# Gated delta-rule attention and expert feed-forward on one core: the correction of a 128x128 inverse summed in the PSUM bank of its first product

## The chip, the cores and the metric

One core of one Trainium2 chip. The metric is the device time of one execution in microseconds (us). The kernel before took 1452.8 us (median of 3 runs, 1451.58 to 1452.94).

## The reference, cut to what matters

Tokens: 2 sequences of 512, 256 features each. A gated delta-rule attention with 16 key heads and 32 value heads of width 128, then a layer norm, a feed-forward of 12 experts (3 chosen per token), and a second layer norm. The attention projects, convolves over 4 taps, applies SiLU, normalises q and k, and runs per value head the recurrence

```
St = St * exp(g_t)
kv = k_t . St
delta = (v_t - kv) * beta_t
St = St + k_t (outer) delta
o_t = q_t . St
```

and then multiplies the normalised output by SiLU(z) and projects it with W_out.

## The kernel before, in words

The kernel walks over 16 "pairs" (one key head n with its two value heads). The recurrence is done in chunks of 128 tokens: 2 sequences x 4 chunks x 2 value heads = 16 matrices (index u) of 128x128 per pair. For each a unit triangular matrix A (strictly lower part in `aT`, split in a float16 high part `aH` and a low part `aL`) has to be inverted. That is done in groups g of four matrices (0 to 3) or halves h of eight:

- steps `st`, `x0`, then five levels of `y`, `p`, `turn` build an approximate inverse `X0` and its transpose `Z0` in float16;
- `res` (L633) forms the residual of that inverse in a PSUM bank, with 12 matmuls; ScalarE takes its high part `res0` (L873), VectorE its low part `res1` (L1083);
- `once` (L645) multiplies `res0` by `Z0`, four matmuls into a bank of its own; ScalarE copies it to SBUF as float16 (L877) and the bank is free;
- `Z` (L654) sums in another bank, for each of the four matrices, `res0 x once`, `res1 x Z0`, `res0 x Z0` and `Z0` itself (through an identity): 16 matmuls at lines 660 to 663; ScalarE copies the sum into `Z` (L881).

`Z` is then used by `solve` (L697), on the chain `ks`, `solve`, `su`, `ks` of the next chunk, which carries the state `St` from chunk to chunk. `pdl`, `qs` give the output, `z` (L666) is the projection of the gate, which ScalarE evacuates with a SiLU (L885), `weigh` multiplies on VectorE, `high` and `low` split the product in two float16 parts, `oT` turns it by DMA, `op` (L725) is the output projection, added up by VectorE. Front of a pair: `proj` (L521) fills the fixed banks 0 and 1, ScalarE copies with the last tap (L788), and `tap` on VectorE adds the other three (L1016); `silu`, `tok`, `v`, `kT`, `kk`, `decay`, `aT`, `unit`, `aH`, `aL` follow. `sq1` are eight small squares on ScalarE (L815).

The order of all of it is written out by hand. `FIRST` covers the start up to pair 0's end, `ORDER` is repeated 12 times (for w = 1 to 12, with steps of pairs w, w+1 and w+2 in one copy), `LAST` covers pairs 13 to 15. Every engine goes through the same list and does those steps that are its own, in that order, so each queue is in order; between engines semaphores decide. `BANK` gives each step that writes PSUM one of the banks 2 to 7. A bank has two semaphores: `full` (TensorE has filled it) and `free` (it has been evacuated). Before a step fills its bank, `take` makes TensorE wait until all earlier uses of this bank in the list are free:

```
            b, k = place(n, step, x)
            if after(k, 1):
                pe.wait_ge(free[b], k)
```

A later step that has been taken by TensorE's queue stands behind that wait. `is_free(..., taking=...)` waits for other steps' evacuations (the data), leaving out those of the bank being taken. DMA loads of weights are issued by SyncE in list order, and wait for the splits of the weights before.

In `ORDER` before, TensorE's sequence around the gate projection is: `tok` 0, `tok` 1, `turn` (4,0) (bank 2), `z` 0 (bank 3), `z` 1 (bank 4), `z` 2 (bank 7), `y` (4,1) (bank 2), `turn` (3,1), `proj` 3, `p` (4,1), `kT` 0, `z` 3, and around the correction: `res` 0, `op` 0, `proj` 0, `once` 0, `res` 1, `op` 1, `res` 2, `Z` 0, `once` 2, `op` 2, `decay` 1, `op` 3, then the next copy with `kk` 0, `kk` 1, `Z` 2, `once` 1, `res` 3, `kk` 2, `solve` 0, `decay` 2, `Z` 1, `st` 0 (bank 2, which is also that of `res` 3), `su` 0, `st` 1, `pdl` 0, `decay` 3, `ks` 1. ScalarE's is `proj` 2, `sq1`, `turn` (4,0), `z` 0, `z` 1, `silu` 2. VectorE's at the start of the copy is `kk` 0, `aT` 0, `kk` 1, `aT` 1, `split` z, `split` out, `res` 3, `kk` 2, `st` 0, `su` 0.

After the attention the feed-forward runs (from some 1100 us on); the change does not touch it.

Of the kernel before, what the change touches and what calls it, by code (L numbers as in the profile page):

```python
# [14 lines left out]
P = 128  # L15
# [52 lines left out]
    (1, "p", (3, 1)), (2, "tap", 2), (2, "sq1", 1), (0, "weigh", 0),
    (2, "tok", 0), (2, "tok", 1), (1, "turn", (4, 0)), (0, "z", 0),
    (0, "z", 1), (2, "silu", 2), (0, "high", 0), (0, "z", 2),  # L70
    (0, "low", 0), (0, "low", 1), (0, "oT", 3), (1, "y", (4, 1)),
    (0, "weigh", 1), (1, "turn", (3, 1)), (2, "proj", 3), (1, "p", (4, 1)),
    (0, "high", 1), (2, "kT", 0), (0, "z", 3), (2, "kT", 1),
    (2, "v", (0, 1)), (2, "tap", 3), (1, "turn", (4, 1)), (2, "silu", 3),
    (2, "v", (0, 0)), (0, "weigh", 2), (0, "weigh", 3), (0, "high", 2),
    (1, "res", 0), (0, "high", 3), (0, "op", 0), (2, "proj", 0),
    (1, "once", 0), (2, "tap", 0), (1, "res", 1), (0, "op", 1),
    (0, "low", 2), (0, "low", 3), (1, "res", 2), (1, "Z", 0),
    (1, "once", 2), (1, "kd", 1), (2, "silu", 0), (1, "aL", 3),
# [50 lines left out]
    (1, "silu", 1), (0, "aL", 2), (0, "p", (4, 0)), (0, "norm", 0),  # L130
    (1, "gl", 1), (0, "y", (3, 1)), (0, "split", "out"), (1, "proj", 2),
    (1, "sq1", 1), (0, "aL", 3), (0, "p", (3, 1)), (0, "kd", 1),
    (1, "silu", 2), (0, "pT", 3), (1, "tap", 2), (1, "tok", 0),
# [3 lines left out]
    (1, "unit", 1), (0, "turn", (4, 0)), (1, "pT", 1), (0, "res", 0),  # L137
    (0, "res", 1), (0, "turn", (4, 1)), (0, "res", 2), (1, "aL", 0),
    (1, "kT", 0), (0, "split", "z"), (1, "silu", 3), (2, "load", "qkv"),
    (0, "once", 0), (1, "tap", 0), (1, "proj", 0), (0, "once", 1),  # L140
# [1765 lines left out]
```

## Time and profile before

| | |
|---|---|
| median of 3 runs | 1452.8 us |
| the profiled execution's own time | 1452.13 us |
| its span | 1450.4 us |
| TensorE (PE) busy | 1386.4 us, 96% of the span |
| VectorE (DVE) busy | 1085.8 us, 75% |
| ScalarE (ACT) busy | 1049.7 us, 72% |
| GpSimd (POOL) busy | 697.1 us, 48% |
| mean granted TensorE clock | 0.982 |
| one middle pair, from 834.41 to 898.32 us | 63.91 us |

A matmul is pipelined: its row in the trace lasts longer than the time until the next one starts, so a busy TensorE may still be issuing slower than it could, and what a matmul costs is read from start to start. Times in the rows are us from the start of the span.

### The profile page before, as it was taken

To read this page: it belongs to the slowest core of one execution; us is meant where nothing else is said; L and a number is where in the kernel's file an instruction comes from. 1 tells how busy PE (TensorE), PEld (TensorE's weight loads), DVE (VectorE), ACT (ScalarE), POOL (GpSimd) and SP (SyncE) were. 2 spreads that over 40 slices of the span, in tenths; PEclk is the share of its full clock that TensorE was granted. 3 is DMA by queue.
4 is the path that set the end of the run, shared out by engine and by line. 5 is a ranking of instruction groups with operands and counts; after the bars stand their busy time and mean duration, and the time that the engine had idled before them with its cause. 6 is when DMAs were issued, how large, how long until landed. Compare 5 with 4: busy or idle time off the path is not lost.

```text
span 1450.4 us, 36480 instructions
## 1 busy us (share of the span) xinstructions
PE 1386.4 (96%) x14236; PEld 1114.9 (77%) x14236; DVE 1085.8 (75%) x1926; ACT 1049.7 (72%) x2114; POOL 697.1 (48%) x619
## 2 busy tenths in 40 slices
PE   5689999999999999999999999999978999999996
PEld 3568888898888889798888979888865567667676
DVE  5678999999999999999999999998865512213225
ACT  5777887878788787878888887887755465564651
POOL 0545555446564545556454555545315454353440
PEclk8899999999999999999999999999998999999998
DMA  3000202011020211102030110201131112112100
GB/s 118 16 1 2 67 3 58 24 38 38 24 60 2 60 24 38 38 25 59 2 60 18 44 38 24 60 2 39 32 101 39 56 37 73 38 37 73 37 1 29
DMA packets 100992, 55.76 MB, mean 38 GB/s; under 512 B 74572, under 2 KB 93016, under 8 KB 100824
## 3 DMA queue, kind: packets, MB, share of 16 engines
q1 hardware_dynamic: 100824, 53.43, 14.2%
q8 instruction: 116, 1.90, 0.5%
q14 instruction: 52, 0.43, 0.1%
HBM read 35.59 MB, written 1.05 MB: 25 GB/s over the span
## 4 chain that ended last, share of the span: by engine, by line
PE 89%; DVE 5%; ACT 2%; issue 2%; DMA 1%; POOL 0%; SPq 0%; POOLq 0%; DVEq 0%; ACTq 0%
PE bank L532 11%; PE bank L1486 11%; PE bank L1469 11%; PE bank L687 6%; PE bank L733 5%; PE bank L674 5%; PE bank L704 4%; PE bank L722 4%; PE bank L713 3%; PE bank L622 2%; PE bank L614 2%; PE bank L630 2%; PE bank L582 2%; PE bank L558 2%; PE bank L583 2%; DVE con L1023 2%
## 5 line engine op out<-in xcount | busy, mean ns | idle before, releaser
L1023 DVE SCALAR_TENSOR_TENSOR con<-bank,taps,con 128x1022 f32<-128x1022 f32 (+2 forms) x192 | 245.4, 1278 | 19.9 <-ACT con L802 15.3
L1808 POOL TENSOR_TENSOR h<-h 128x512 f16<-128x512 f32 x120 | 142.5, 1192 | 159.7 <-ACT h L1586 147.7
L532 PE MATMUL bank<-x,qkv 128*128 128x512 f16 x768 | 183.5, 390 | 6.5 <-DVE con L1023 6.5
L1179 POOL TENSOR_TENSOR gl<-const_sb,gc 128x512 f16<-128x512 f32 x128 | 129.9, 1040 | 120.3 <-DVE gc L1033 75.2
L1585 ACT ACTIVATE h<-bank,b 128x512 f32<-128x512 f32 x120 | 82.5, 687 | 119.0 <-PE bank L1469 115.8
L1469 PE MATMUL bank<-y,w 128*128 128x512 f16 x720 | 163.2, 386 | 1.7 <-ACT h L1586 1.4
L1486 PE MATMUL bank<-w,h 128*128 128x256 f16 x1440 | 159.9, 273 | 0.0
L1486 PEld LDWEIGHTS bank<-w,h 128*128 128x128 f16 x1440 | 140.9, 98 | 18.4
L532 PEld LDWEIGHTS bank<-x,qkv 128*128 128x128 f16 x768 | 73.4, 100 | 88.5 <-issue 8.7
L1469 PEld LDWEIGHTS bank<-y,w 128*128 128x128 f16 x720 | 70.2, 99 | 90.6 <-ACT h L1586 8.1
L1214 POOL TENSOR_TENSOR oo<-oo 128x512 f16<-128x512 f32 x64 | 74.2, 1170 | 122.0 <-ACT oo L930 122.0
L1081 DVE TENSOR_TENSOR X<-X,bank 128x512 f16<-128x512 f16 x160 | 109.0, 682 | 16.1 <-PE bank L622 14.7
L1399 DVE SCALAR_TENSOR_TENSOR w<-w,w 128x1280 f16<-128x1280 f32 x12 | 17.8, 1490 | 134.1 <-ACT w L1387 134.1
L871 ACT ACTIVATE Z<-bank 128x512 f16<-128x512 f32 x160 | 96.4, 604 | 23.7 <-PE bank L630 23.7
L1072 DVE TENSOR_TENSOR Y<-bank,ymask 128x512 f16<-128x512 f32 x160 | 109.4, 685 | 2.9 <-PE bank L614 2.3
L802 ACT ACTIVATE con<-bank,taps 128x512 f32<-128x512 f32 x128 | 85.4, 687 | 30.8 <-PE bank L532 30.6
L1206 POOL TENSOR_TENSOR kd<-k_tok,gc 128x512 f32<-128x512 f32 x48 | 50.0, 1043 | 112.0 <-PE bank L713 112.0
L733 PE MATMUL bank<-out,sqo 128*128 128x256 f16 x768 | 96.7, 277 | 7.2 <-ACT zs L889 5.5
L1187 POOL TENSOR_TENSOR pT<-kkm,decay 128x512 f32<-128x512 f32 x64 | 88.0, 1376 | 17.4 <-issue 12.8
L1709 DVE SCALAR_TENSOR_TENSOR facc<-bank,gcol,facc 128x256 f32<-128x256 f32 x88 | 38.5, 479 | 76.6 <-PE bank L1486 76.6
L674 PE MATMUL bank<-z,x 128*128 128x256 f16 x768 | 89.6, 273 | 1.4 <-ACT zs L889 0.8
L733 PEld LDWEIGHTS bank<-out,sqo 128*128 128x128 f16 x768 | 73.3, 99 | 22.1 <-issue 8.7
(222 smaller groups left out, 3858.2 us busy)
## 6 DMA issues: line engine op xcount, KB each, us to landing
w<-in_w SPq DMA_DIRECT2D x24, 640.0 KB, 4.4
w_qkv<-in_W_qkvz SPq DMA_DIRECT2D x16, 512.0 KB, 4.3
w_out<-in_W_out SPq DMA_DIRECT2D x16, 256.0 KB, 3.0
...
sqo<-oo SPq DMA_TRANSPOSE x64, 2.7
...
```

The lines of the kernel that those rows point to most:

```text
L532: last = mm(bank[:, b], qkv16[:, w, a, t * P:(t + 1) * P], x16[:, x, a, b * S:(b + 1) * S], start=(a == k == 0), stop=(a == HT - 1 and k = ...
L674: last = mm(out[:, j * 256:(j + 1) * 256], x16[:, x, a, m * P:(m + 1) * P], z16[:, w, a, :], start=(a == k == 0), stop=(a == HT - 1 and k ...
L733: last = mm(out[:, j * H:(j + 1) * H], oT[:, g % 2, o, 2 * j + r], out16[:, w, r, :], start=(r == i == 0), stop=(r == R - 1 and i == len(P ...
L871: freed(do(dst, src, ACT.Copy), "turn", lh)
L1023: stt(out=out, in0=bank[:, 0:B, 0:S - k], scalar=taps[:, par, t, TAPS - 1 - k:TAPS - k], in1=out, op0=ALU.mult, op1=ALU.add).then_inc(tap_ ...
L1072: freed(tt(Y[:, h], at_bank("y", lh).rearrange("p (u k) -> p u k", u=8), ymask[:, l].unsqueeze(1).broadcast_to([P, 8, P // 2]), ALU.mult), ...
L1081: freed(tt(x, x, at_bank("p", lh).rearrange("p (q b) -> p q b", b=b), ALU.subtract), "p", lh)
L1179: last = tt(gl[:, g % 2, k].rearrange("p (m r) d -> p m r d", m=2), upper.unsqueeze(1).unsqueeze(1).broadcast_to([P, 2, R, P]), gc[:, par, ...
L1187: tt(pT[:, par, 4 * g:4 * g + 4].rearrange("p (m r) d -> p m r d", m=2), kkm[:, g % 2, :, 1].unsqueeze(2).broadcast_to([P, 2, R, P]), deca ...
L1469: last = mm(h_bank(n, k), w1_16[:, n % 2, w, a, t * P:(t + 1) * P], y16[:, x, a, h * S:(h + 1) * S], start=(a == i == 0), stop=(a == HT - ...
L1486: last = mm(o_bank(k)[:, j * H:(j + 1) * H], h16[:, n % 2, h, t, m * P:(m + 1) * P], w2_16[:, n % 2, w, t, :], start=(t == i == 0), stop=( ...
L1808: tt(h16[:, n % 2, 1, t, at], h32[:, k % H32], h16[:, n % 2, 0, t, at], ALU.subtract).then_inc(h_low, 1)
```

## The change

`once` of group g keeps its bank until the inverse is finished. The four products of `once` are written with the start flag on the first alone (so that the other three, and later the correction, are added or written without clearing the bank's state), ScalarE copies them to SBUF as before but does not free the bank; the step `Z` then adds three matmuls per matrix into the same bank, and the fourth, `res0 x Z0`, is gone, since `once` has left it there. `Z` has no bank of its own any more. Two semaphores per group, `once_ready` and `z_full`, take the place of the bank's. `solve` waits for the bank of `once`.

```diff
 apply_once (TensorE)
-                last = mm(out[:, j * P:(j + 1) * P], res0[:, g, j], Z0[:, 4 * g + j], start=True, stop=True)
+                last = mm(out[:, j * P:(j + 1) * P], res0[:, g, j], Z0[:, 4 * g + j], start=(j == 0), stop=True,
+                          skip_group_check=True)
 finish_z (TensorE)
-            is_free(pe, n, ("res", g), ("once", g), taking=("Z", g))
-            out = take(n, "Z", g)
+            pe.wait_ge(once_ready[g], n + 1)
+            is_free(pe, n, ("res", g))
+            out = at_bank("once", g)
-                mm(out[:, at], res0[:, g, j], once[:, g % 2, j], start=True, stop=False)
-                mm(out[:, at], res1[:, g, j], Z0[:, u], start=False, stop=False)
-                mm(out[:, at], res0[:, g, j], Z0[:, u], start=False, stop=False)
-                last = mm(out[:, at], ident16[:], Z0[:, u], start=False, stop=True)
-            filled(last, "Z", g)
+                mm(out[:, at], res0[:, g, j], once[:, g % 2, j], start=False, stop=False, skip_group_check=True)
+                mm(out[:, at], res1[:, g, j], Z0[:, u], start=False, stop=False, skip_group_check=True)
+                last = mm(out[:, at], ident16[:], Z0[:, u], start=False, stop=True, skip_group_check=True)
+            last.then_inc(z_full[g], 1)
 solve (TensorE)
-                needs += [("Z", c // 2), ("Z", 2 + c // 2)]
+                needs += [("once", c // 2), ("once", 2 + c // 2)]
 apply_once, finish_z (ScalarE)
-            freed(do(once[:, g % 2], quads(at_bank("once", g)), ACT.Copy), "once", g)
+            do(once[:, g % 2], quads(at_bank("once", g)), ACT.Copy).then_inc(once_ready[g], 1)
-            freed(do(Z[:, 4 * g:4 * g + 4], quads(at_bank("Z", g)), ACT.Copy), "Z", g)
+            freed(do(Z[:, 4 * g:4 * g + 4], quads(at_bank("once", g)), ACT.Copy), "once", g)
```

The lists `FIRST`, `ORDER` and `LAST` are written anew, with the same steps in other places, and `BANK` in part: `once` 0 from bank 2 to 5, `once` 2 from 5 to 3, `y` (4,1) from 2 to 3; the entries of `Z` are gone. TensorE's sequence in `ORDER`, where it differs:

```diff
 around the gate projection (bank in brackets)
-turn 4,0 [2]  z 0 [3]  z 1 [4]  z 2 [7]  y 4,1 [2]  turn 3,1  proj 3  p 4,1  kT 0  z 3
+turn 4,0 [2]  z 0 [3]  y 4,1 [3]  z 1 [4]  z 2 [7]  turn 3,1  proj 3  kT 0  p 4,1  z 3
 around the correction
-res 0  op 0  proj 0  once 0  res 1  op 1  res 2  Z 0  once 2  op 2  decay 1  op 3
+res 0  res 1  op 0  proj 0  op 1  once 0  res 2  Z 0  once 2  op 2  decay 1  op 3
 start of the copy
-kk 0  kk 1  Z 2  once 1  res 3  kk 2  solve 0  decay 2  Z 1  st 0
+kk 0  kk 1  once 1 [6, as kk 0]  Z 2  res 3  kk 2  solve 0  decay 2  Z 1  st 0
 later
-turn 0,0  st 3  Z 3  p 1,0     solve 2  turn 1,0  p 0,1  v 1,1  y 2,0
+turn 0,0  Z 3  st 3  p 1,0     solve 2  p 0,1  v 1,1  y 2,0  turn 1,0
```

VectorE in `ORDER`: `split` z, `res` 3, `split` out in place of `split` z, `split` out, `res` 3; `res` 1 ahead of `op` 0. ScalarE: `once` 1 and `Z` 2 ahead of the splits, `res` 3 between them. GpSimd: the same cycle. In the new `FIRST`, TensorE does `proj` 2 ahead of `tok` 0 and `norm` after `kk` 1, the loads of z and of pair 1 stand earlier, and z's steps are `z` 0, `z` 1, `z` 2, `turn` 3,1, `turn` 4,0, `y` 4,1. In the new `LAST`, pair 13 has `z` 0, `z` 1, `turn` 4,0, `z` 2, `y` 4,1, and pair 15 has `once` 2, `Z` 2, `op` 2 (of 14), `solve` 0, `res` 3, `su` 0, `once` 1, `pdl` 0, `ks` 1, `qs` 1, `solve` 1, `once` 3, `Z` 1, `su` 1, `pdl` 1, `Z` 3, `ks` 2, `op` 3 (of 14), `solve` 2, where it had `once` 2, `op` 2, `Z` 2, `res` 3, `solve` 0, `op` 3, `su` 0, `pdl` 0, `ks` 1, `Z` 1, `solve` 1, `qs` 1, `su` 1, `pdl` 1, `once` 3, `ks` 2, `Z` 3, `solve` 2.

## Rows read from the trace of the kernel before

**Rows 1.** The page: span, busy time of the engines, granted clock in slices.
```profile
span 1450.4 us, 36480 instructions
...
PE 1386.4 (96%) x14236; PEld 1114.9 (77%) x14236; DVE 1085.8 (75%) x1926; ACT 1049.7 (72%) x2114; POOL 697.1 (48%) x619
...
PEclk8899999999999999999999999999998999999998
```

**Rows 2.** The page: the chain that ended last, by engine.
```profile
PE 89%; DVE 5%; ACT 2%; issue 2%; DMA 1%; POOL 0%; SPq 0%; POOLq 0%; DVEq 0%; ACTq 0%
```

**Rows 3.** Windows, the middle and one pair: busy us (instructions), clock, DMA share.
```profile
84.00:1087.00 1003.00, 985.89 (x11462) 845.48 (x11460) 916.10 (x1606) 805.87 (x1731) 515.40 (x453) 1.00 0.15 35
...
834.41:898.32 63.91, 63.79 (x745) 54.76 (x745) 59.73 (x105) 52.49 (x113) 34.14 (x30) 1.00 0.14 35
```

**Rows 4.** Timeline of TensorE, one step Z: start us, us, line, operation.
```profile
866.94 0.22 PE L660 MATMUL bank<-once,res 128*128 128x128 f16 x1
...
867.78 0.22 PE L663 MATMUL bank<-Z,ident 128*128 128x128 f16 x1
867.83 0.39 PE L651 MATMUL bank<-Z,res 128*128 128x128 f16 x4
```

**Rows 5.** Timeline of TensorE around the gate projection of one pair.
```profile
848.69 0.40 PE L630 MATMUL bank<-unit_cols,X 128*128 128x64 f16 x8
848.92 4.09 PE L674 MATMUL bank<-z,x 128*128 128x256 f16 x36
852.85 0.40 PE L614 MATMUL bank<-X,aH 128*128 128x64 f16 x8
```

**Rows 6.** Timeline of ScalarE, and tile zs: min/median/max ns.
```profile
848.53 0.28 ACT L824 ACTIVATE sq<-bank 128x128 f32<-128x128 f32 x1
...
850.54 0.65 ACT L871 ACTIVATE Z<-bank 128x512 f16<-128x512 f32 x1
851.02 1.32 ACT L889 ACTIVATE zs<-bank 128x512 f32<-128x512 f32 x2
...
L889 ACT ACTIVATE zs<-bank x2: 597/627/657, 851.0 to 851.7; 128x512 f32<-128x512 f32 x2
```

**Rows 7.** Timeline, a copy of ScalarE that waited for TensorE.
```profile
873.75 0.22 PE L663 MATMUL bank<-Z,ident 128*128 128x128 f16 x1
...
874.01 0.60 ACT L883 ACTIVATE Z<-bank 128x512 f32<-128x512 f32 x1 [0.26 <-PE bank L663]
```

**Rows 8.** The chain in order of time: TensorE released by ScalarE.
```profile
1074.58 0.60 ACT dl L904
1075.18 0.04 issue
1075.23 1.17 PE bank L722 x8
```

**Rows 9.** Timeline of TensorE and VectorE ahead of st 0.
```profile
877.33 0.68 DVE L1085 SCALAR_TENSOR_TENSOR res<-bank,res 128x512 bf16<-128x512 f32 x1
...
877.81 0.22 PE L663 MATMUL bank<-Z,ident 128*128 128x128 f16 x1
...
878.15 0.38 PE L593 MATMUL bank<-ident,aH 128*128 128x128 f16 x4
```

**Rows 10.** Timeline: the state of chunk 0 on VectorE, and ks 1.
```profile
879.53 0.69 DVE L1102 COPY St<-bank 128x512 f32<-128x512 f32 x1 [0.27 <-PE bank L713]
...
880.93 1.03 PE L687 MATMUL bank<-St,kT 128*128 128x256 f32 x4
```

**Rows 11.** Waits of TensorE, the longest in total: us, times, longest.
```profile
PE bank L532 <- DVE con L1023: 6.5, 4, 2.7
```

**Rows 12.** Timeline of TensorE in the last pair, solve 0 to ks 1.
```profile
1053.32 1.13 PE L704 MATMUL bank<-v_tok,Z 128*128 128x128 f32 x8 [0.17 <-issue]
1054.28 1.47 PE L733 MATMUL bank<-out,sqo 128*128 128x256 f16 x12
...
1057.43 1.13 PE L687 MATMUL bank<-St,kT 128*128 128x256 f32 x4
```

**Rows 13.** Windows, TensorE idle and the stretch after it, twice: clock third from last.
```profile
85.80:88.53 2.73, 0.02 (x2) 0.01 (x1) 2.60 (x3) 0.98 (x9) 1.61 (x2) 1.00 0.03 6
88.53:92.00 3.47, 3.47 (x26) 2.08 (x27) 1.89 (x3) 2.87 (x5) 3.47 (x4) 1.00 0.00 0
1076.00:1087.00 11.00, 5.80 (x52) 4.72 (x50) 9.26 (x17) 5.76 (x9) 5.38 (x3) 1.00 0.09 22
1087.00:1093.80 6.80, 5.42 (x25) 3.61 (x26) 3.89 (x11) 1.58 (x3) 3.04 (x4) 0.50 0.38 85
```

More of the change, by code:

```diff
@@ L68 @@
[L68 to L79, printed above, removed]
+    (0, "aL", 3), (1, "kk", 0), (1, "load", "z"), (1, "aT", 0),
+    (1, "kk", 1), (0, "once", 1), (0, "Z", 2), (1, "aT", 1),
+    (0, "split", "z"), (0, "res", 3), (0, "split", "out"), (1, "aH", 0),
[5 rows of a table added]
+    (0, "solve", 1), (0, "once", 3), (1, "p", (0, 0)), (1, "unit", 1),
@@ new lines @@
+    (0, "qs", 1), (1, "st", 2), (1, "aL", 0), (0, "su", 1),
+    (1, "pT", 1), (1, "aL", 1), (1, "y", (1, 0)), (0, "pdl", 1),
+    (1, "unit", 2), (1, "aH", 3), (2, "load", "qkv"), (1, "turn", (0, 0)),
[10 rows of a table added]
+    (0, "sum", 0), (0, "sum", 1), (2, "proj", 1), (1, "p", (2, 1)),
+    (1, "load", "out"), (1, "pT", 3), (1, "y", (4, 0)), (0, "solve", 3),
+    (2, "tap", 1), (2, "gl", 2), (0, "power", 0), (1, "turn", (3, 0)),
+    (2, "decay", 0), (1, "y", (3, 1)), (0, "pdl", 3), (1, "p", (4, 0)),
+    (0, "sum", 2), (0, "sum", 3), (0, "sqo", 2), (0, "oT", 2),
@@ L80 @@
+    (2, "silu", 3), (2, "v", (0, 0)), (0, "weigh", 2), (0, "weigh", 3),
+    (0, "high", 2), (1, "res", 0), (1, "res", 1), (0, "high", 3),
+    (0, "op", 0), (2, "proj", 0), (2, "tap", 0), (0, "op", 1),
+    (1, "once", 0), (0, "low", 2), (0, "low", 3), (1, "res", 2),
+    (1, "Z", 0), (1, "once", 2), (1, "kd", 1), (2, "silu", 0),
     (0, "op", 2), (2, "decay", 1), (0, "op", 3),
@@ L130 @@
[L130 to L133, printed above, removed]
[3 rows of a table removed]
[L137 to L140, printed above, removed]
[15 rows of a table removed]
@@ L167 @@
-    (0, "oT", 1), (1, "p", (3, 1)), (2, "tap", 2), (0, "weigh", 0),
-    (2, "tok", 0), (1, "turn", (4, 0)), (2, "tok", 1), (0, "weigh", 1),
-    (0, "z", 0), (0, "z", 1), (1, "load", "out"), (0, "high", 0),
-    (0, "z", 2), (1, "turn", (3, 1)), (2, "silu", 2), (0, "low", 0),
[4 rows of a table removed]
-    (0, "high", 2), (2, "tap", 0), (2, "v", (0, 0)), (0, "high", 3),
-    (2, "proj", 0), (0, "low", 1), (0, "op", 1), (2, "silu", 3),
-    (1, "turn", (4, 1)), (1, "res", 2), (1, "Z", 0), (0, "low", 2),
-    (1, "load", "z"), (1, "once", 2), (0, "op", 2), (2, "silu", 0),
@@ new lines @@
+    (1, "tap", 1), (0, "turn", (2, 1)), (0, "split", "out"), (0, "p", (3, 1)),
+    (1, "decay", 0), (0, "turn", (3, 0)), (1, "silu", 1), (1, "load", "z"),
+    (0, "p", (4, 0)), (1, "proj", 2), (1, "tap", 2), (1, "sq1", 1),
+    (0, "y", (4, 1)), (1, "tok", 0), (0, "turn", (3, 1)), (1, "tok", 1),
+    (1, "silu", 2), (1, "proj", 3), (0, "aL", 2), (0, "p", (4, 1)),
+    (1, "v", (0, 1)), (0, "turn", (4, 0)), (1, "tap", 3), (1, "kT", 0),
+    (0, "res", 0), (0, "res", 1), (1, "v", (0, 0)), (1, "silu", 3),
@@ new lines @@
+    (0, "res", 2), (0, "turn", (4, 1)), (1, "proj", 0), (0, "once", 0),
+    (0, "aL", 3), (1, "gl", 1), (1, "tap", 0), (1, "kT", 1),
+    (2, "split", "qkv"), (0, "kd", 1), (0, "Z", 0), (1, "v", (1, 0)),
+    (0, "once", 2), (0, "res", 3), (1, "silu", 0), (0, "Z", 2),
[25 rows of a table added]
+    (2, "silu", 1), (0, "sqo", 3), (0, "power", 0), (0, "sum", 3),
+    (1, "norm", 0), (2, "proj", 2), (1, "p", (3, 1)), (2, "tap", 2),
+    (0, "weigh", 0), (2, "tok", 0), (2, "sq1", 1), (2, "tok", 1),
[3 rows of a table added]
+    (2, "kT", 1), (0, "weigh", 2), (2, "tap", 3), (0, "weigh", 3),
@@ L181 @@
+    (0, "high", 1), (0, "low", 0), (1, "p", (4, 1)), (0, "high", 2),
+    (2, "v", (0, 1)), (1, "res", 0), (2, "v", (0, 0)), (1, "res", 1),
+    (0, "high", 3), (0, "op", 0), (2, "tap", 0), (0, "low", 1),
+    (1, "once", 0), (2, "proj", 0), (0, "op", 1), (1, "turn", (4, 1)),
+    (0, "low", 2), (0, "low", 3), (1, "Z", 0), (1, "res", 2),
+    (2, "silu", 3), (0, "op", 2), (2, "silu", 0), (1, "once", 2),
+    (1, "pT", 3), (2, "decay", 1), (2, "gl", 2), (0, "op", 3),
+    (1, "load", "out"),
 ]
@@ L183 @@
 LAST = [
-    (15, "load", "qkv"), (14, "kk", 0), (14, "gl", 3), (14, "load", "out"),
-    (14, "aT", 0), (13, "Z", 2), (14, "kk", 1), (13, "split", "out"),
-    (13, "once", 1), (14, "aT", 1), (13, "res", 3), (13, "solve", 0),
[19 rows of a table removed]
-    (15, "gc", 0), (14, "turn", (1, 1)), (15, "proj", 1), (13, "sum", 1),
[3 rows of a table removed]
-    (14, "turn", (3, 0)), (15, "decay", 0), (14, "turn", (2, 1)), (13, "pdl", 3),
-    (15, "silu", 1), (13, "sqo", 3), (14, "norm", 0), (14, "p", (4, 0)),
-    (14, "y", (3, 1)), (15, "proj", 2), (14, "oT", 2), (13, "power", 0),
@@ L213 @@
-    (13, "sum", 3), (14, "p", (3, 1)), (15, "tap", 2), (15, "sq1", 1),
-    (14, "oT", 3), (13, "weigh", 0), (15, "tok", 0), (15, "tok", 1),
-    (14, "turn", (3, 1)), (13, "z", 0), (14, "y", (4, 1)), (13, "z", 1),
-    (13, "high", 0), (15, "silu", 2), (13, "weigh", 1), (15, "tap", 3),
[4 rows of a table removed]
-    (15, "v", (0, 0)), (13, "low", 1), (13, "high", 2), (14, "once", 0),
-    (15, "tap", 0), (13, "low", 2), (15, "proj", 0), (13, "high", 3),
-    (15, "silu", 3), (13, "op", 1), (14, "res", 1), (14, "res", 2),
@@ new lines @@
+    (13, "split", "z"), (14, "unit", 0), (14, "aH", 0), (14, "unit", 1),
[7 rows of a table added]
+    (14, "turn", (0, 0)), (14, "aL", 1), (14, "y", (1, 0)), (15, "load", "qkv"),
[3 rows of a table added]
+    (14, "load", "out"), (13, "qs", 2), (13, "kd", 2), (13, "solve", 2),
[7 rows of a table added]
+    (14, "p", (2, 1)), (15, "tap", 1), (14, "turn", (3, 0)), (13, "solve", 3),
+    (15, "decay", 0), (14, "turn", (2, 1)), (14, "norm", 0), (14, "kd", 0),
+    (13, "pdl", 3), (14, "y", (3, 1)), (13, "oT", 0), (13, "oT", 1),
+    (14, "p", (4, 0)), (13, "power", 0), (15, "silu", 1), (13, "sqo", 3),
@@ new lines @@
+    (15, "proj", 2), (13, "sum", 3), (15, "sq1", 1), (14, "p", (3, 1)),
+    (15, "tap", 2), (13, "weigh", 0), (15, "tok", 0), (15, "tok", 1),
+    (13, "z", 0), (13, "z", 1), (13, "weigh", 1), (14, "turn", (4, 0)),
+    (15, "silu", 2), (13, "z", 2), (14, "y", (4, 1)), (15, "tap", 3),
+    (13, "high", 0), (14, "turn", (3, 1)), (15, "proj", 3), (13, "weigh", 2),
[3 rows of a table added]
+    (15, "proj", 0), (14, "once", 0), (14, "turn", (4, 1)), (13, "low", 1),
+    (14, "aL", 2), (13, "high", 3), (15, "silu", 3), (15, "tap", 0),
@@ new lines @@
+    (14, "sum", 3), (15, "turn", (2, 1)), (14, "sqo", 3), (15, "aL", 2),
+    (14, "z", 0), (15, "pT", 2), (15, "y", (3, 1)), (14, "kd", 2),
+    (14, "z", 1), (15, "p", (4, 0)), (15, "p", (3, 1)), (15, "norm", 0),
+    (15, "turn", (4, 0)), (15, "turn", (3, 1)), (14, "weigh", 0), (14, "weigh", 1),
[3 rows of a table added]
+    (15, "res", 0), (15, "turn", (4, 1)), (15, "v", (1, 0)), (15, "load", "z"),
+    (14, "high", 2), (14, "weigh", 3), (15, "res", 1), (15, "kd", 0),
[3 rows of a table added]
+    (15, "solve", 0), (15, "res", 3), (15, "su", 0), (15, "once", 1),
@@ new lines @@
+    (15, "pdl", 0), (15, "sqo", 0), (15, "ks", 1), (15, "qs", 1),
+    (14, "low", 0), (15, "solve", 1), (15, "once", 3), (15, "Z", 1),
+    (15, "su", 1), (15, "pdl", 1), (15, "Z", 3), (14, "low", 1),
+    (15, "ks", 2), (14, "low", 2), (14, "op", 3), (15, "sum", 0),
+    (15, "split", "out"), (15, "solve", 2), (15, "qs", 2), (15, "su", 2),
[3 rows of a table added]
+    (15, "sqo", 2), (14, "low", 3), (15, "sqo", 3), (15, "pdl", 3),
+    (15, "z", 0), (15, "sum", 2), (15, "sum", 3), (15, "z", 1),
+    (15, "high", 0), (15, "weigh", 0), (15, "power", 0), (15, "low", 0),
```

101 lines of the change are left out of this document (48 added, 53 removed), and 249 rows, old and new, of tables (BANK, FIRST, LAST, ORDER).

## The prediction

> **What bounds the kernel now.** I read the page first. TensorE is busy 96% of the span and works at full clock in nearly all slices [rows 1], and the chain that ended last lies on it for 89% [rows 2]. A share over the whole says little of a stage, so I took windows. In the middle, 84 to 1087 us, TensorE is busy 985.89 of 1003 us; one pair lasts 63.91 us and TensorE is busy 63.79 of them, VectorE 59.73, ScalarE 52.49 [rows 3]. So in the middle TensorE's issue is the bound: what is taken from it is taken from the time, and what makes it wait is added. VectorE has 4 us of air per pair, so it is the next bound. The profiled execution took 1452.13 us for a span of 1450.4, so 1.7 us lie around the span; it is 0.7 us under the median of 1452.8, and my sum is made against 1452.13 and then raised by that 0.7.
>
> **What is removed.** The step Z loses one of its four matmuls per matrix, the one at L662. What a matmul costs is the time until the next starts: the 16 of a step Z start at 866.94 and the next step at 867.83 [rows 4], which is 0.89 us or 56 ns each. A step becomes 0.67 us. Four steps per pair make 16 matmuls or 0.89 us per pair, 14.3 us over 16 pairs. The Trainium skill, page TensorE: Matmul & The Clock Gate, section "Back-to-back issue gap", gives about 81 ns for a matmul of 128 columns in a stream with weight loads; by it the sum would be 20.7 us, an estimate from that page. The trace disagrees: 56 ns with a weight load ahead of each, and the row decides. The start flag, the two semaphores per group and the ScalarE copy that no longer frees a bank cost no instruction on a busy engine that I can see; I take 0, and for eight small waits 0 to 0.05 us per pair at most, as the 0.04 us of a handover [rows 8] shows. DMAs are the same ones; the loads move to places where the weights are still in time by a whole step list, cost 0 as long as `split` doesn't stand waiting for them.
>
> **What the new places cost in the middle.** I went through TensorE's new sequence and asked for every step how much TensorE work lies between the filling of what it waits for and itself. Before, the smallest distance in a middle copy is 0.9 us (about an evacuation of 0.6 with its handovers). After, these fall under it.
>
> (a) `y` (4,1) now has bank 3 and stands directly behind `z` 0, which fills bank 3: distance zero. It must wait until ScalarE has evacuated `z` 0. In the trace `z` 0 starts at 848.92 [rows 5]; its 12 of 36 matmuls, at (852.85 - 848.92)/36 = 0.109 us, are issued by 850.23. ScalarE is late there: its squares start at 848.53 and it copies `turn` (4,0) at 850.54 and starts the SiLU of `z` 0 at 851.02, 0.66 us long [rows 6], so it ends at 851.68. The order on ScalarE and the steps ahead of `z` 0 are the same after. With a handover of 0.04 us [rows 8] TensorE goes on at 851.72 instead of 850.23: 1.5 us. If ScalarE were idle at that point, the cost would be the 0.16 us by which the last matmul outlasts its issue, 0.04 us until a copy starts [rows 7], 0.6 us and the same back: 0.9 us at the least. The upper bound is 1.6, with a weight load that can't be drawn ahead. I take 1.5, since the ScalarE rows ahead of it stay. Behind it in TensorE's queue stand `z` 1, `z` 2, `proj` 3 and all the rest, so the whole copy shifts.
>
> (b) `Z` 0 follows `once` 0 with only `res` 2 (12 matmuls, 0.67 us) between, and needs ScalarE's copy of it: 0.16 + 0.04 + 0.60 + 0.04 + up to 0.1 [rows 7, 8] less 0.67 is 0.25 us, between 0 and 0.3.
>
> (c) `once` 1 takes the bank of `kk` 0 one step later (0.9 us): 0.05 us, between 0 and 0.1.
>
> (d) `st` 0 gains: before, its bank's last user `res` 3 was evacuated by VectorE from 877.33 to 878.01, behind both splits, and TensorE, whose last matmul of Z 1 started at 877.81, started `st` 0 at 878.15 in place of 877.86 [rows 9]: 0.29 us, gone, as `res` 3 now stands ahead of one split. Between 0 and 0.29; I take 0.29.
>
> (e) VectorE does the same 59.73 us, but `p` (4,1) now stands behind `kT` 0 and holds up tap 3 on VectorE, and `res` 1 goes ahead of tap 0, so VectorE gets some 0.3 to 0.9 us later than TensorE's shift. At `ks` 1 TensorE needs `St`, which was ready at 880.22 against a start at 880.93 [rows 10], 0.7 us of air. I take 0.15 us, between 0 and 0.5.
>
> Per pair: -0.89 + 1.5 + 0.25 + 0.05 - 0.29 + 0.15 = +0.77 us; bounds -0.89 + 0.9 - 0.29 = -0.28 and -0.89 + 1.6 + 0.3 + 0.1 + 0.5 = +1.61. The other swaps (`Z` 3 ahead of `st` 3, `turn` (1,0) three steps later, `once` in other banks) leave 0.9 us or more and cost 0. `ORDER` runs 12 times: 12 x 0.77 = +9.2 us (-3.4 to +19.3).
>
> **The ends.** In `FIRST` and `LAST`, `y` (4,1) stands 2.8 us or more behind `z` 0, so (a) isn't there. Four pairs' worth of removed matmuls, 3.6 us, are left; those of pair 15 stand partly in a stretch where the chain of the state waits anyway, so I count 2.9. In `LAST`, from `solve` 0 to `ks` 1 of pair 15 there were 4.11 us with `op` 3 of pair 14 in between [rows 12]; after, `res` 3 is in its place and `once` 1 behind: about 3.8, and `op` 3 goes where TensorE waited for VectorE; against that `Z` 2 stands directly behind `once` 2 and waits 0.9, but `op` 2 then covers its copy. I take -1.0, between -2.5 and +1. In `FIRST` the pace is that of the taps (TensorE waits 6.5 us for them in four places [rows 11]); `proj` 2 ahead of `tok` 0 lets it start some 2 us sooner, but the ScalarE copy stands behind the gate terms and the squares now come later. I take 0, between -3 and +3. Ends together: -3.9 us (-8 to +1).
>
> Sum: +9.2 - 3.9 = +5.3 us. 1452.13 + 5.3 = 1457.4, with the 0.7 to the median 1458; I give 1457.5.
>
> **Rivals.** First, **the wait is hidden**: the evacuation of `z` 0 comes in time, or TensorE's waits elsewhere in the pair absorb it, and the removed matmuls are gained in full: 1452.8 - 14.3 - 1 = 1437.5. For it: nothing else on TensorE got longer. Against: ScalarE's rows stand where they stand, and in the pair TensorE was busy all but 0.12 us, so there is nothing to absorb. Chance 0.13.
>
> Second, **the ends decide**: the middle comes out near its lower half (ScalarE less late, so 1.1 us for (a), and (b), (c), (e) near 0: +0.1 per pair, +1) and the lists of the ends give 3 to 8 us: 1446 to 1452. For it: in the head TensorE idles much, and loads and taps stand earlier. Against: the taps' pace on VectorE stays. Chance 0.25.
>
> Third, **the clock falls in the wait**. Each pair gets one idle stretch of some 1.3 us. After 5.5 us idle the granted clock was 0.50 of full (1.2 GHz) for 6.8 us; after 2.7 us idle at 85.8 it stayed at 1.00 (2.4 GHz) [rows 13]. Were it to fall in every copy for half of such a stretch, 3.4 us at half pace, 1.7 us would be lost, 12 x 1.7 = 20 us more: 1478. The row with 2.7 us speaks against it. Chance 0.04. The Trainium skill, same page, section "What's actually happening", says that activity releases the throttle and idleness brings it back; the two pairs of windows agree with it in kind.
>
> The forecast itself has 0.58: slower by 1 to 17 us.
>
> **How the numbers follow.** A measurement of this kernel can tell about 0.2%, 2.9 us, from no change. Under 1449.9: the first rival, and somewhat under half of the second, 0.24. From 1449.9 to 1455.7: the rest of the second and the lowest part of the forecast, 0.21. Above: 0.55. The range runs from 1445, the middle's lower bound with the ends' mean, to 1466, the forecast with +1.4 per pair; outside lie the first rival, most of the third and the extremes, 0.2.
>
> **What would show it.** A middle pair of 64.7 us in place of 63.91, 729 matmuls in it in place of 745. In the waits, TensorE's L614 behind ScalarE's SiLU at L889 (line numbers moved) some 12 times, about 1.3 us idle each; the gate projection split in 12 and 24 matmuls with the gap between. Small idle times ahead of the first matmul of Z 0. `st` 0 no longer held by `res` 3. The clock at 1.00 through the middle. I'd be wrong if that wait were short (ScalarE's SiLU ending within 0.9 us of the issue of `z` 0), if the pair took 63.0 us, or if the clock dipped in each pair.

## The result and the profile after

The kernel after took **1459.58 us** (median of 5 runs, 1459.07 to 1463.76), the kernel before 1452.35 us on the same chip (5 runs): a ratio of 1.0056, 95% interval 1.0042 to 1.0071. The change made the kernel 0.6% slower, by 7.2 us. The profiled execution of after took 1459.07 us, 6.94 more than that of before.

The page of after, against [rows 1]:

```profile
span 1457.3 us, 36014 instructions
...
PE 1375.7 (94%) x13980; PEld 1100.0 (75%) x13980; DVE 1097.4 (75%) x1926; ACT 1050.0 (72%) x2114; POOL 701.5 (48%) x619
...
PEclk8799999999999999999999999999998999999998
```

There are 256 matmuls fewer (14236 to 13980), and TensorE's busy time fell by 10.7 us, while the span grew by 6.9. So TensorE now stands idle for 17.6 us more than before. The windows say where: the same middle pair as in [rows 3], and below it the stretch from pair 0's `kk` 0 to pair 1's, in both kernels (after first).

```profile
817.55:882.24 64.69, 63.23 (x730) 53.75 (x729) 60.75 (x106) 52.43 (x114) 34.11 (x31) 1.00 0.16 35
49.18:107.36 58.18, 44.39 (x492) 33.24 (x493) 43.08 (x56) 39.85 (x82) 22.37 (x22) 0.88 0.07 20
```

```profile
49.48:105.19 55.71, 43.49 (x520) 32.34 (x521) 42.33 (x55) 39.64 (x83) 23.64 (x23) 0.94 0.04 11
```

A pair went from 63.91 to 64.69 us. TensorE was idle 0.12 us in it before; now it is 1.46, at full clock. The waits name one place for nearly all of it. TensorE's waits of after, in us in total, times, and the longest:

```profile
PE bank L615 <- ACT zs L901: 17.3, 12, 1.4
PE bank L533 <- DVE con L1035: 7.8, 4, 3.3
...
PE bank L663 <- ACT once L890: 2.1, 3, 0.8
```

L615 is `y` (L614 before), L901 the SiLU of the gate projection (L889 before): 12 waits of 1.44 us, one in each copy of `ORDER`. TensorE's timeline there, and ScalarE's beside it:

```profile
858.15 0.40 PE L631 MATMUL bank<-unit_cols,X 128*128 128x64 f16 x8
858.38 1.47 PE L676 MATMUL bank<-z,x 128*128 128x256 f16 x12
861.30 0.39 PE L615 MATMUL bank<-X,aH 128*128 128x64 f16 x8 [1.44 <-ACT zs L901]
861.53 2.78 PE L676 MATMUL bank<-z,x 128*128 128x256 f16 x24
```

```profile
857.99 0.28 ACT L826 ACTIVATE sq<-bank 128x128 f32<-128x128 f32 x1
...
860.02 0.65 ACT L876 ACTIVATE Z<-bank 128x512 f16<-128x512 f32 x1
860.50 0.66 ACT L901 ACTIVATE zs<-bank 128x512 f32<-128x512 f32 x1
863.04 0.60 ACT L901 ACTIVATE zs<-bank 128x512 f32<-128x512 f32 x1 [1.89 <-PE bank L676]
```

The 36 matmuls of [rows 5] are now 12, a gap, and 24. `z` 0's last matmul is issued at 858.38 + 12 x 0.109 = 859.69. ScalarE is still at the squares, copies `turn` (4,0) at 860.02 and starts the SiLU at 860.50; it ends at 861.16, and `y` (4,1) starts at 861.30. That is 1.61 us late, and ScalarE then waits 1.89 us for the next gate block: TensorE and ScalarE take turns where they had overlapped.

The other edits, in the same copy. Ahead of `st` 0 nothing is waited for now, since `res` 3 stands ahead of `split` out (TensorE, then VectorE; before: [rows 9]):

```profile
888.69 0.22 PE L665 MATMUL bank<-Z,ident 128*128 128x128 f16 x1
888.74 0.28 PE L594 MATMUL bank<-ident,aH 128*128 128x128 f16 x2
```

```profile
886.48 1.07 DVE L1019 SCALAR_TENSOR_TENSOR z<-w_z,z 128x512 f16<-128x512 f32 x1
887.47 0.68 DVE L1097 SCALAR_TENSOR_TENSOR res<-bank,res 128x512 bf16<-128x512 f32 x1
888.07 0.73 DVE L1025 SCALAR_TENSOR_TENSOR out<-w_out,normw,out 128x512 f16<-128x512 f32 x1
```

And two small gaps are new, each ahead of a step that the change put too close behind what fills its bank or its operand: `Z` 0, which has only `res` 2 between itself and the `once` 0 whose copy it needs, and `once` 1, which has only `kk` 1 between itself and the `kk` 0 whose bank it takes:

```profile
877.91 0.22 PE L643 MATMUL bank<-ident,minus 128*128 128x128 f16 x1
878.15 0.23 PE L663 MATMUL bank<-once,res 128*128 128x128 f16 x1
...
883.87 0.39 PE L584 MATMUL bank<-qT,kT 128*128 128x128 f32 x2
884.24 0.38 PE L652 MATMUL bank<-Z,res 128*128 128x128 f16 x4
```

From start to start this is 0.24 us where the pace of such a matmul is 0.056, so 0.18 lost, and 0.37 us for two f32 matmuls of 0.11 each, so about 0.14 lost.

There is a third one, at `kk` 0. It needs the SiLU of `silu` 0 (L814, L812 before), which needs `tap` 0 on VectorE. Here are ScalarE and TensorE in after, then in the kernel before:

```profile
881.08 1.06 ACT L814 ACTIVATE qT<-con 128x1024 f32<-128x1024 f32 x1 [0.96 <-DVE con L1035]
880.80 1.47 PE L735 MATMUL bank<-out,sqo 128*128 128x256 f16 x12
882.24 0.46 PE L583 MATMUL bank<-kT 128*128 128x128 f32 x2
```

```profile
869.11 1.06 ACT L812 ACTIVATE qT<-con 128x1024 f32<-128x1024 f32 x1
869.82 1.47 PE L733 MATMUL bank<-out,sqo 128*128 128x256 f16 x12
871.13 0.39 PE L582 MATMUL bank<-kT 128*128 128x128 f32 x2
```

Before, the SiLU was over at 870.17, 0.96 us ahead of `kk` 0, and `kk` 0 followed the 12 matmuls of `op` 3 at their pace. In after the SiLU is over at 882.14, `kk` 0 starts 0.10 us behind it, 0.13 later than the pace of `op` 3 (12 x 0.109 = 1.31 us) would have it, and a further 0.07 us goes between its first two matmuls, so that `kk` 1 starts 0.97 us after `kk` 0 instead of 0.89. Together 0.20 us per pair.

### The profile page after: what moved, and what is told of

Its sections match the earlier page's. It is cut to its first block, busy times and chain, and to the rows that moved or that the text cites. A ratio compares the mean times of both kernels' runs of the same rounds, so it can differ in the third digit from the quotient of the medians.

```text
span 1457.3 us, 36014 instructions
## 1 busy us (share of the span) xinstructions
PE 1375.7 (94%) x13980; PEld 1100.0 (75%) x13980; DVE 1097.4 (75%) x1926; ACT 1050.0 (72%) x2114; POOL 701.5 (48%) x619
## 4 chain that ended last, share of the span: by engine, by line
PE 79%; DVE 10%; ACT 7%; issue 3%; POOL 0%; DMA 0%; SPq 0%; POOLq 0%; ACTq 0%; DVEq 0%
PE bank L1498 11%; PE bank L1481 10%; PE bank L533 9%; PE bank L689 6%; PE bank L735 5%; PE bank L676 4%; DVE con L1035 4%; PE bank L706 3%; PE bank L724 3%; PE bank L715 3%; PE bank L615 2%; PE bank L583 2%; PE bank L623 2%; ACT sq L826 2%; PE bank L559 2%
## 5 line engine op out<-in xcount | busy, mean ns | idle before, releaser
L1226 POOL TENSOR_TENSOR oo<-oo 128x512 f16<-128x512 f32 x64 | 75.8, 1186 | 144.3 <-ACT oo L942 144.3
```

## The experiments

E1 undoes the one edit of the change that the profile accuses; E2 to E4 vary it or take it apart from the rest, and E5 to E10 are E1 with one thing more (E9 with two). Each was timed against the kernel before on the same chip (its median there was 1451.88 to 1452.65 us). "Pair" is the distance of `kk` 0 from one middle pair to the next.

| | median, us (runs) | ratio to before (95%) | pair, us | `kk` 0 of pair 1 at |
|---|---|---|---|---|
| before | 1452.35 (5) | 1 | 63.91 | 105.19 |
| after | 1459.58 (5) | 1.0056 (1.0042 to 1.0071) | 64.69 | 107.36 |
| E1 `y` (4,1) back | 1442.89 (4) | 0.9934 (0.9915 to 0.9953) | 63.08 | 112.70 |
| E2 `y` (4,1) in bank 2 | 1462.02 (4) | 1.0063 (1.0048 to 1.0078) | 64.18 | 111.03 |
| E3 before, `y` (4,1) early | 1473.75 (4) | 1.015 (1.0133 to 1.0166) | 65.47 | 107.47 |
| E4 new sum, old lists | 1461.24 (4) | 1.0062 (1.0047 to 1.0077) | 63.89 | 107.79 |
| E5 `once` places back | 1443.86 (4) | 0.9926 (0.9905 to 0.9948) | 63.00 | 112.92 |
| E6 fourth matmul again | 1458.06 (5) | 1.0026 (1.0008 to 1.0043) | 63.78 | 112.5 |
| E7 old `FIRST` | **1439.02** (4) | 0.9905 (0.9891 to 0.992) | 63.08 | 105.23 |
| E8 splits ahead of `res` 3 | 1450.77 (10) | 0.9984 (0.9972 to 0.9996) | 63.66 | 112.17 |
| E9 E5 and E7 together | 1440.83 (4) | 0.9918 (0.9901 to 0.9934) | 62.98 | 107.70 |
| E10 `norm` later | 1441.1 (4) | 0.9915 (0.9901 to 0.993) | 63.08 | 109.10 |

**E1: `y` (4,1) behind `z` 2 again.** The kernel after; bank 3 is kept.

```diff
 ORDER, around the gate projection
-z 0 [3]  y 4,1 [3]  z 1 [4]  z 2 [7]
+z 0 [3]  z 1 [4]  z 2 [7]  y 4,1 [3]
```

> The changed kernel with y (4,1) moved back behind z 2 in the repeated list, its bank (3) kept. My theory, that TensorE's wait for the SiLU of z 0 (1.61 us in the profile of the changed kernel) costs 12 times its length: a pair of 63.1 to 63.3 us in place of 64.69, 17 to 19 us less than the changed kernel, 1441 to 1443. The rival, that VectorE or the order around the correction sets the new period and the wait only stands where another one would appear: pair 64 us or more, 1452 or more.

A pair of E1, against that of after above:

```profile
806.72:869.80 63.08, 63.06 (x730) 53.76 (x729) 59.84 (x106) 52.53 (x114) 34.01 (x31) 1.00 0.16 35
```

```profile
847.55 4.09 PE L676 MATMUL bank<-z,x 128*128 128x256 f16 x36
851.48 0.40 PE L615 MATMUL bank<-X,aH 128*128 128x64 f16 x8
```

The gate's 36 matmuls are one block again, TensorE is idle for 0.02 us, and the pair is 1.61 us shorter, what the timeline of after had given. 12 x 1.61 = 19.3 us; of this its profiled execution shows 14.3 (1459.07 to 1444.78), as its head came out 5.3 us longer with an unchanged `FIRST` (see E10). One place in a list of steps makes the difference between 0.6% slower and 0.7% faster.

**E2: only the bank.** The kernel after, with `y` (4,1) still directly behind `z` 0.

```diff
 BANK
-("y", (4, 1)): 3
+("y", (4, 1)): 2
```

> The changed kernel with only the bank of y (4,1) changed, 3 to 2 (the bank of turn (4,0), one step ahead of z 0, which ScalarE copies just before its SiLU of z 0). If it is the bank that makes TensorE wait and ScalarE's lateness that sets the length: the wait shrinks from 1.6 to 1.1 us, since the copy ends 0.5 us ahead of the SiLU, a pair of 64.2 us, 5 to 7 us less, some 1453.5. If the new place alone cost the time whatever the bank: no change, 1459.5.

The wait got a new owner, and a slightly smaller size. E2's waits, and its timeline:

```profile
PE bank L615 <- ACT Z L876: 13.9, 13, 2.6
```

```profile
862.14 0.39 PE L615 MATMUL bank<-X,aH 128*128 128x64 f16 x8 [0.94 <-ACT Z L876]
```

Bank 2 was filled by `turn` (4,0), one step further back, and ScalarE copies that directly ahead of the SiLU. The pair takes 64.18 us, so 1.10 more than in E1 in place of 1.61. It isn't the bank alone: at this point of the list both banks that were tried are still full, and ScalarE comes to them late, behind its squares. In the total the expected 5 to 7 us did not come, and E2 gains nothing on after: its head is 3.7 us longer, and one wait of 2.6 us stands at the transition from pair 1 to 2.

**E3: the kernel before, with that edit alone.**

```diff
 ORDER and BANK of before
-z 0 [3]  z 1 [4]  z 2 [7]  y 4,1 [2]
+z 0 [3]  y 4,1 [3]  z 1 [4]  z 2 [7]
```

> The kernel before with only y (4,1) put directly behind z 0 in the repeated list and into bank 3, the correction untouched. If the wait is the cost, a pair grows by 1.5 to 1.6 us to 65.5, and with the one such place of the last list the time by 19 to 21 us: 1471 to 1474. The rival, that the wait hurts only in the changed kernel, where VectorE has less air: under 1460.

```profile
PE bank L614 <- ACT zs L889: 18.8, 13, 1.7
```

```profile
826.17:891.64 65.47, 63.92 (x747) 54.69 (x746) 60.74 (x105) 52.25 (x114) 33.94 (x32) 1.00 0.15 34
```

(The first row is from E3's waits, the second from its windows.) 1.56 us more per pair than before, 18.7 us over 12 copies, and 21.9 us in the median. The price of the place is the same with the old correction as with the new one, so (a) owes nothing to the summing in one bank.

**E4: the summing alone.** The correction as after (three matmuls per matrix, `once`'s bank kept), with the lists and banks of before. Three entries had to change so that a kept bank has no other user in between.

```diff
 BANK of before: no entries for Z;  once 0: 2 -> 3;  decay 1: 5 -> 3
 LAST of before: (15, once 1) moved behind (14, op 2)
```

> The summing in the bank of once alone: the lists and banks of the kernel before, except once 0 and decay 1 in bank 3, and once 1 of the last pair behind op 2 of pair 14, so that no bank is asked for while once holds it. If a removed matmul is worth its 56 ns of issue: 16 x 12 in the middle give 0.89 us a pair, 63.0 us, less up to 0.3 if Z 0 or st 0 waits longer; 12 to 14.5 us less than before, 1438 to 1440.5. If the correction's new waits eat it: 1448 or more.

This was the surprise. 16 matmuls fewer per pair, and the pair takes 63.89 us where it took 63.91. E4's window, then TensorE and VectorE ahead of `st` 0:

```profile
751.20:815.09 63.89, 63.27 (x731) 53.89 (x729) 59.83 (x105) 52.46 (x114) 34.15 (x32) 1.00 0.14 35
```

```profile
758.22 0.38 PE L593 MATMUL bank<-ident,aH 128*128 128x128 f16 x4 [0.49 <-DVE res L1096]
```

```profile
756.36 1.12 DVE L1024 SCALAR_TENSOR_TENSOR out<-w_out,normw,out 128x512 f16<-128x512 f32 x1
757.40 0.68 DVE L1096 SCALAR_TENSOR_TENSOR res<-bank,res 128x512 bf16<-128x512 f32 x1
```

TensorE arrives earlier, and VectorE, which has `res` 3 behind both splits, does not: what `st` 0 loses, from start to start, went from 0.29 to 0.66 us (the row's 0.49 us counts from the end of the last matmul). A further 0.26 stands ahead of `once` 0 and 0.18 ahead of `once` 2. These rows show what came just before the two:

```profile
807.24 0.69 DVE L1096 SCALAR_TENSOR_TENSOR res<-bank,res 128x512 bf16<-128x512 f32 x1 [0.52 <-ACT res L881]
808.08 0.38 PE L651 MATMUL bank<-Z,res 128*128 128x128 f16 x4
...
811.15 0.60 ACT L881 ACTIVATE res<-bank 128x512 f16<-128x512 f32 x1 [1.29 <-PE bank L642]
811.80 0.40 PE L651 MATMUL bank<-Z,res 128*128 128x128 f16 x4
```

`once` 0 starts behind VectorE's `res` 0, whose bank (3) it takes in E4 and took in no other kernel here; so this wait is E4's own. `once` 2 starts 0.05 us behind ScalarE's copy of `res` 2, now that `Z` 0 between the two is 0.22 us shorter. Together 0.37 + 0.26 + 0.18 = 0.81 of the 0.89 us were given back. On top of that come stretches that the banks of this kernel lengthen (68.29 us for pair 1, where TensorE waits once 4.2 us for VectorE at `once`, and 66.91 us from pair 14 to 15), which is why E4 is 0.6% slower in total. So in E4, with the old lists and its three changed entries, the removed matmuls shorten no middle pair. Of the three waits that eat the gain only the one at `st` 0 is VectorE's `res` 3 behind the splits.

**E8: that edit by itself.** E1, with VectorE's old order.

```diff
 ORDER, VectorE
-split z  res 3  split out
+split z  split out  res 3
```

> The kernel of e1_y41_back with split out ahead of res 3 again on ScalarE and VectorE. My term (d): st 0 waits for the bank of res 3 again. With Z 2 and Z 1 shorter the wait is 0.6 rather than 0.29 us: a pair of 63.5 to 63.7 us, 5 to 7 us more than e1_y41_back. If the place of the split doesn't matter: 63.08.

```profile
PE bank L594 <- DVE res L1097: 5.1, 12, 0.4
```

The pair takes 63.66 us (+0.58) and the median rises by 7.9 us on E1. The moved `split`, which looked worth 0.29 us by the trace of before, is worth twice that once TensorE is faster. The pair is still 0.25 us shorter than before, so with the new places of TensorE's steps part of the gain stays even behind both splits.

**E6: what the removed matmul is worth.** E1, with `res0 x Z0` added to the sum a second time, so that there are four matmuls per matrix again.

```diff
 finish_z
                 mm(out[:, at], res1[:, g, j], Z0[:, u], start=False, ...
+                mm(out[:, at], res0[:, g, j], Z0[:, u], start=False, ...
                 last = mm(out[:, at], ident16[:], Z0[:, u], start=False, ...
```

> The kernel of e1_y41_back with the fourth matmul of each matrix issued again into the sum (res0 x Z0 is then added twice). This is the price of the removed work under the new order. If the middle is bound by TensorE's issue: 16 x 56 ns = 0.89 us a pair, 63.97 us, 12 to 14 us more than e1_y41_back. If VectorE bounds the new period: under 63.5.

```profile
815.95:879.73 63.78, 63.76 (x746) 54.72 (x745) 59.43 (x105) 52.63 (x114) 33.80 (x31) 1.00 0.14 35
```

0.70 us in this pair, or 44 ns for each of the 16, and not 0.89. The steps show where the rest is: each `Z` is 0.22 us longer, as the start-to-start pace says, but `kk` 1 follows `kk` 0 by 0.89 us instead of 0.97, and 0.11 us is made up between `op` 2 and the next `kk` 0. That is the wait of `kk` 0 for the SiLU: in E1 it starts 0.10 us behind the SiLU's end, as in after, and in E6 TensorE comes 0.20 us after it and doesn't wait. Not every pair of E6 is so short: three of them take 64.23 to 64.51 us, the 12 copies together 10.4 us more than E1's, and the median is 15.2 us above E1's (13.3 in the profiled executions), where 16 x 0.89 would be 14.3. So the price over the whole kernel is about what the pace says. By the figure of the Trainium skill that the prediction weighed, 81 ns each (page TensorE: Matmul & The Clock Gate, section "Back-to-back issue gap"), E6 would, as an estimate from that page, have lost 1.3 us per pair; the pair above disagrees, and the measurement decides.

**E5: the small gaps.** E1, with `once` 0 ahead of `op` 1, and `Z` 2 ahead of `once` 1.

```diff
 ORDER
-op 1  once 0  res 2  Z 0        kk 1  once 1  Z 2
+once 0  op 1  res 2  Z 0        kk 1  Z 2  once 1
```

> The kernel of e1_y41_back with two more moves in the repeated list: once 0 ahead of op 1, once 1 behind Z 2. My reading of the step starts: Z 0's wait for once 0 (0.18 us) and once 1's for the bank of kk 0 (0.22 us with kk 1's late start) go, a pair 62.7 us in place of 63.08, 4 to 5 us less than e1_y41_back. The rival, VectorE as the next bound (59.7 busy of 63.08): the waits appear elsewhere, pair 63.0 to 63.1.

Both gaps went, and a new one of 0.18 us stands ahead of `once` 2, which starts 0.05 us behind ScalarE's copy of `res` 2, as in E4. The 0.20 us at `kk` 0 stayed. The pair takes 63.00 us, 0.08 less and not the 0.4 that I had expected, so about 1 us over 12 copies, which the medians cannot tell from nothing (1443.86 against 1442.89).

**E7, E9, E10: the head.** E7 is E1 with the old `FIRST` (three steps in it placed so that it fits the new `ORDER`: `aL` 3 of pair 1 is left to `ORDER`, `Z` 2 goes ahead of `kT` 1, `once` 0 of pair 1 behind `v` (0,0) of pair 2). E9 has E5's `ORDER` and E7's `FIRST`. E10 is E1 with one step later in the new `FIRST`:

```diff
 FIRST
-kk 1  aT 1  norm 0  kk 2
+kk 1  aT 1  kk 2
 ...
-p 4,0  proj 2 (of pair 1)
+p 4,0  norm 0  proj 2 (of pair 1)
```

> The kernel of e1_y41_back with the first list of the kernel before (aL 3 of pair 1 left to the repeated list; Z 2 of pair 0 ahead of kT 1, once 0 of pair 1 behind v (0,0), since banks are held longer). If the new first list costs the head 2 to 7 us (kk 0 of pair 1 at 107.4 and 112.7 us in two kernels with it, 105.2 in the kernel before, with the clock at half more often): kk 0 of pair 1 at 103 to 106 us and 2 to 7 us less than e1_y41_back, 1436 to 1440. If that is chance of the clock: no difference.

> The parts that helped, together: y (4,1) back behind z 2, the old first list (e7_old_first), and once 0 and once 1 moved (e5_correction_places, which gained 0.08 us a pair of the 0.4 it aimed at). If the two are independent: pair 63.0 us, kk 0 of pair 1 at 105, 0.5 to 1.5 us less than e7_old_first, 1437.5 to 1438.5, 13 to 15 us less than the kernel before.

> The kernel of e1_y41_back with norm 0 of pair 0, in the new first list between kk 1 and kk 2, moved back behind p (4,0), where the old list has it. In e1_y41_back its 16 products take from 52.9 to 56.2 us at the half clock, ahead of kk 2 and st 0, on which the first inverse waits. If that place costs the head: kk 2 starts at 53 us, kk 0 of pair 1 at 107 to 110 in place of 112.7 us, 2 to 5 us less than e1_y41_back. If the rest of the new list or the clock is the cause: 112 us and no difference.

E7 has the lowest median of all, 1439.02 us (1438.36 to 1440.3), 0.95% under the kernel before; its ratio's interval overlaps those of E1, E5, E9 and E10. Its `kk` 0 of pair 1 starts at 105.23, as before. From 49 to 70 us, the windows of after, E1 and E7:

```profile
49.00:70.00 21.00, 17.18 (x168) 15.17 (x169) 14.68 (x22) 13.81 (x27) 8.50 (x8) 0.76 0.04 6
```

```profile
49.00:70.00 21.00, 17.67 (x121) 15.73 (x121) 9.99 (x16) 11.06 (x23) 8.41 (x8) 0.58 0.00 1
```

```profile
49.00:70.00 21.00, 15.45 (x202) 12.47 (x202) 16.44 (x25) 13.58 (x27) 8.66 (x9) 0.93 0.09 27
```

After and E1 have the same `FIRST`, and yet a granted clock of 0.76 and 0.58, with 168 and 121 matmuls in the same 21 us. E7 has 0.93 and 202 matmuls. Ahead of that stretch TensorE idles for some 5 us in each (from 44 to 49 us it is busy 0.07 us in after, 0.28 in E1, 0.30 in E7), waiting for the last tap and its SiLU. After this the new `FIRST` has sixteen f32 matmuls of `norm` ahead of `kk` 2, on the head's way: their row of E1 (3.41 us for the 16, at the low clock) and of after (1.84):

```profile
52.93 3.41 PE L542 MATMUL bank<-ones,sq 128*128 128x1 f32 x16
```

```profile
52.57 1.84 PE L542 MATMUL bank<-ones,sq 128*128 128x1 f32 x16
```

E10 took them from there, and `kk` 2 came at 52.68 us in place of 56.20, `kk` 0 of pair 1 at 109.10 in place of 112.70. The median is 1.8 us under E1's, but the two intervals of the ratio overlap, and the clock was higher too (0.64 against 0.50 from 49 to 57 us). That `norm` costs the head something is likely and not shown; what sets the clock there isn't settled. E7 and E9 have the same `FIRST` and differ as well (105.23 and 107.70 us), by more than the 1 us that E9's `ORDER` should save: E7's median is 1.8 us the lower, and the gain expected of E9 did not come.

All profiled executions side by side say more than two of them. With the old `FIRST`, `kk` 0 of pair 1 came at 105.19 and 105.23 us where the clock from 49 to 57 us was 0.79 and 0.82 (before, E7), and at 107.47 to 107.79 us where it was 0.61 to 0.65 (E3, E4, E9). With the new `FIRST` it came at 107.36 us with 0.79 (after), and at 111.03 to 112.92 us with 0.50 (E1, E2, E5, E6, E8). So at the same clock in that stretch the new start is some 2.1 us later (one execution of after against those of before and E7; from 57 to 75 us its clock was lower too, 0.81 against 1.00), and at a lower clock either start is later still.

## Why the prediction was right, and where it was not

The forecast was 1457.5 us with a range of 1445 to 1466, slower with 0.55; it came to 1459.58. The kernel's middle did what the likeliest case said, nearly term by term. One pair, in us:

| term | predicted | measured | read from |
|---|---|---|---|
| removed matmuls | -0.89 | -0.89 in the steps; -0.70 net | starts of the steps `Z`; E6 |
| (a) `y` (4,1) behind `z` 0 | +1.5 | +1.61 | after's timeline; E1 (-1.61), E3 (+1.56) |
| (b) `Z` 0 behind `once` 0 | +0.25 | +0.18 | after's timeline; gone in E5 |
| (c) `once` 1 in `kk` 0's bank | +0.05 | +0.14 | after's timeline; gone in E5 |
| (d) `st` 0's wait | -0.29 | -0.29 | after's timeline; E8 (+0.58 without it) |
| (e) VectorE late | +0.15, at `ks` 1 | 0 at `ks` 1, +0.20 at `kk` 0 | `ks` 1 starts 2.78 us after `st` 0 in both kernels; `kk` 0 behind the SiLU of tap 0, after's timeline |
| sum | +0.77 | +0.78 | pairs of 63.91 and 64.69 us |

**(a)** decided the sign, as forecast, and E1 shows it: without it the same kernel is 0.66% faster than before. The working behind it held as well: ScalarE's steps ahead of the SiLU stayed where they were, so the upper of the two bounds was nearly met (1.6), not the 0.9 of an idle ScalarE. What was missing of 1.61 against 1.5 is 0.14 us between the SiLU's end at 861.16 and TensorE's first matmul at 861.30, where I had counted the 0.04 of [rows 8].

**(b), (c)** were of the right kind, and (c) was nearly three times as large as I had put it. **(e)** was right in kind, near in size and wrong in place. I had said that `res` 1 ahead of `tap` 0 makes VectorE late, and looked for it at `ks` 1, where its air was enough. It came at `kk` 0 of the next pair: the SiLU behind `tap` 0 had 0.96 us of air there before and has none now, and TensorE loses 0.20 us. E3 and E4, which keep the old `ORDER` (E3 but for one step), have 0.96 us or more of that air in the middle pairs. The measured terms, with a wait of 0.10 us at `p` (2,0) that went and that I had not foreseen, add up to +0.85; two starts that were 0.03 us late before and aren't in after leave 0.01 us that is not located. The single terms are off by up to 0.11 us either way, so that the sum came within 0.01 us is luck.

**(d)** was right for this kernel and undersold as a mechanism. I took it as a wait of 0.29 us that goes, a small item between others. E8 shows that it grows as TensorE gets faster, since VectorE's time of delivery does not move: with `res` 3 behind both splits it is 0.58 us, two thirds of what the 16 matmuls had given, and in E4 0.66. The prediction's sentence on the middle, "what is taken from it is taken from the time, and what makes it wait is added", holds only where no step waits for another engine's schedule, and the 0.29 us of [rows 9] was the sign that one did.

**The ends** I put at -3.9 us. The span grew by 6.9 us, and 9.7 of it (I had 9.2) lie between `kk` 0 of pair 1 and that of pair 14, so the ends gave -2.8, split in another way than I had it: the head lost 2.2, pair 14 to 15 gained 1.6 (63.89 to 62.29 us), `kk` 0 of pair 15 to `op` 3 gained 2.6 (97.28 to 94.64), and 0.8 went behind that. In the third of these `solve` 0 to `ks` 1, from 4.11 to 3.97 us (I had said 3.8), has only a small part; most of it, 1.6 us, lies ahead of `solve` 0 (54.38 to 52.80 us from `kk` 0). Here is that last stretch of after, against [rows 12]:

```profile
1062.00 1.06 PE L706 MATMUL bank<-v_tok,Z 128*128 128x128 f32 x8
...
1065.97 1.04 PE L689 MATMUL bank<-St,kT 128*128 128x256 f32 x4
```

The head lost: `kk` 0 of pair 1 came 2.2 us later (107.36 against 105.19), inside my 0 +- 3 but on the wrong side. I had expected the earlier `proj` 2 to help there or do nothing. I had named no mechanism for a loss; `norm` ahead of `kk` 2 (1.84 us in after) is the candidate that E10 leaves. E7 points the same way: with the old `FIRST` the median is 3.9 us under E1's. But the clock has a part in that: the two runs of E1 with a mean granted clock of 0.983 took 1439.71 and 1441.09 us, the two with 0.978 and 0.977 took 1444.69 and 1444.78, and E7's four had 0.984 to 0.986.

**The rivals.** The hidden wait (1437.5, chance 0.13) did not come, but its number is near what the change gives with the wait taken out and the old `FIRST`: E7 reaches 1439.02. The ends didn't decide. The clock did not fall in the middle: 1.00 in the pair of 64.69 us, with 1.44 us idle in each. It was low in the head (0.79 from 49 to 57 us), behind an idle stretch of some 5 us, as it had been before (0.79); that stretch is not the change's.

**The size.** The profiled execution (1459.07) lies 1.7 us above the sum's 1457.4: 0.5 in the middle and 1.1 in the ends, nearly all of it the head's 2.2 us, which the tail did not quite pay for.
